# A graph layer on one Trainium2 core: the in-degree rows by one-hot products in the main loop, and five segments of edges in place of four

## What is computed

```python
h = jnp.maximum(_layernorm(x), 0.0)
in_deg = jnp.minimum(segment_sum(ones, dst, num_nodes), 511)
out_deg = jnp.minimum(segment_sum(ones, src, num_nodes), 511)
sum3d = segment_sum(edge_attr @ W_sum + b_sum, src, num_nodes)
cent_term = sigmoid(centralities @ W_cent + b_cent)
vor_term = sigmoid(voronoi_values @ W_vor + b_vor)
out = x + h + z_in[in_deg] + z_out[out_deg] + cent_term + vor_term + sum3d
```

## Time and profile before

| | |
|---|---|
| three runs | 2472.15, 2475.61, 2476.04 us; median 2475.61 |
| profiled execution, its own time | 2477.0 us |
| its span | 2475.2 us (1.8 us less) |
| main loop | to the last scatter, 2132.4 us |
| first piece of the last segment | 2137.4 us |
| piece 150 of the last segment (first step with a window) | 2259 us |
| last piece | 2457 us |

### The profile page before, as it was taken

How to read it: one execution, slowest core, us unless ns; L and a number is a source line. 1 busy time by engine, 2 the same in 40 slices (tenths; PEclk the granted TensorE clock), 3 DMA queues, 4 the chain that set the end, 5 groups by cost and what they waited for, 6 DMA issues and landing times.

```text
span 2475.2 us, 40112 instructions
## 1 busy us (share of the span) xinstructions
PE 1568.7 (63%) x8689; PEld 1168.9 (47%) x8689; DVE 1655.5 (67%) x5321; ACT 895.0 (36%) x4489; POOL 1852.2 (75%) x1869
## 2 busy tenths in 40 slices
PE   5756666666666432237766765666677766687776
PEld 2234554444454210016555554554565655566655
DVE  8946677878878621549887754444576665698766
ACT  3533333444343533545444433333233333001323
POOL 5777777777777777777777777777777777766786
PEclk7867667766766555559988888777799888899888
DMA  5356544445555553348767776666688777799996
GB/s 141 99 157 197 152 130 129 135 142 158 153 154 156 153 175 106 105 122 234 213 206 213 207 214 187 189 181 183 207 257 236 234 229 216 192 243 222 243 249 187
DMA packets 485071, 451.90 MB, mean 183 GB/s; under 512 B 72407, under 2 KB 444637, under 8 KB 484828
## 3 DMA queue, kind: packets, MB, share of 16 engines
q1 hardware_dynamic: 402782, 300.08, 45.0%
q0 software_dynamic: 78752, 136.44, 17.5%
q10 hardware_dynamic: 3294, 12.80, 1.6%
HBM read 319.28 MB, written 129.59 MB: 181 GB/s over the span
## 4 chain that ended last, share of the span: by engine, by line
POOL 51%; DMA 19%; issue 19%; DVE 4%; PE 3%; ACT 2%; DVEq 1%; SPq 1%; ACTq 0%; POOLq 0%
POOL sorted L528 51%; DMA edge_ring<-in_edge_attr_dram 6%; DMA sorted<-edge_ring,pos_i 6%; DMA edge_ring<-in_L_gnn_z_out_dram,out_i 5%; DMA piece_ring<-sorted 2%; PE bank L1011 2%; ACT junk L863 1%; DVE acc L712 1%; DVE hot_n L685 1%; PE bank L1030 1%; DVE base L800 0%; SPq L423 0%; PE bank L957 0%; DVE gate_normed L751 0%; ACT edge_ring L878 0%
## 5 line engine op out<-in xcount | busy, mean ns | idle before, releaser
L528 POOL DMA_INDIRECT sorted<-edge_ring,pos_i x1660 | 1604.0, 966 | 524.9 <-issue 487.4
L1011 PE MATMUL bank<-piece_ring,hot_n 128*125 128x129 f32 x4920 | 860.6, 326 | 210.3 <-DVE hot_n L685 186.3
L1011 PEld LDWEIGHTS bank<-piece_ring,hot_n 128*125 128x125 f32 x4920 | 772.4, 227 | 348.8 <-DVE hot_n L685 306.3
L685 DVE SCALAR_TENSOR_TENSOR hot_n<-bank,wkey,piece_ring 128x250 f32<-128x250 f32 x1230 | 579.4, 471 | 509.6 <-DMA piece_ring<-sorted 484.6
L863 ACT ACTIVATE junk<-bank,mark_col 128x100 bf16<-128x100 f32 x1664 | 543.4, 337 | 142.9 <-PE bank L988 141.8
L994 PE MATMUL bank<-hot_w,after_b 128*128 128x400 bf16 x416 | 177.6, 427 | 573.6 <-ACT junk L863 568.6
L878 ACT ACTIVATE edge_ring<-key_f 128x5 f32<-128x5 f32 x332 | 69.6, 210 | 1093.3 <-DMA edge_ring<-in_edge_attr_dram 1092.4
L712 DVE TENSOR_TENSOR acc<-bank,acc 125x129 f32 x1230 | 348.3, 283 | 42.5 <-issue 26.5
L994 PEld LDWEIGHTS bank<-hot_w,after_b 128*128 128x128 bf16 x416 | 45.8, 110 | 643.5 <-ACT junk L863 643.3
L863 ACT ACTIVATION_READ_ACCUMULATOR junk<-bank,mark_col 128x1 f32 x1664 | 334.1, 201 | 0.0
L1037 PE MATMUL bank<-hot_dl,hot_dh 128*125 128x100 bf16 x1661 | 199.9, 277 | 27.7 <-DVE hot_dh L620 25.6
(11 more groups left out here) (109 smaller groups left out, 1182.5 us busy)
## 6 DMA issues: line engine op xcount, KB each, us to landing
piece_ring<-sorted SPq DMA_DIRECT2D x1230, 130.0 KB
edge_ring<-in_edge_attr_dram SPq DMA_DIRECT2D x332, 320.0 KB
sorted<-edge_ring,pos_i POOLq DMA_INDIRECT x1660
base<-in_x_dram SPq DMA_DIRECT2D x20, 560.0 KB
out_dram<-base ACTq DMA_DIRECT2D x19, 560.0 KB
out_dram<-base SPq DMA_DIRECT2D x9, 560.0 KB
base<-out_dram SPq DMA_DIRECT2D x9, 560.0 KB
edge_ring<-in_L_gnn_z_out_dram,out_i POOLq DMA_INDIRECT x100, 6.8
```

The lines of the kernel that those rows point to most:

```text
L528: g.indirect_dma_start(rows, bass.IndirectOffsetOnAxis(index, 0), edge_ring[:, slot, at, :], None).then_inc(s_scatter[slot], 16)
L685: v.scalar_tensor_tensor(out=hot_n[:, n % HOT_SLOTS, 0:G, :], in0=iota_ps.unsqueeze(1).to_broadcast([P, G, LOC]), scalar=wkey[:, s % 2, c: ...
L1011: last = t_.matmul(to, hot_n[:, n % HOT_SLOTS, k, :], piece_ring[:, n % PIECE_SLOTS, k, 0:SUM], start=(k == 0), stop=(k == ROW_GROUPS[s] - 1))
```

## The change

It moves the z_in rows into the main loop and cuts the segments anew: 25, 165, 110, 70 and 46 quads. The pieces are 150, 430, 320, 240 and 190 (1330 in all) where they were 150, 470, 360 and 250 (1230); `ahead` is 90 where it was 150. After the histogram is done, the 512 rows of z_in are loaded whole into `dst_parts`, which is free by then. For each window there is a new item `look` in two halves. The first spreads the window's in-degrees over the partitions (one matmul of 125 columns), and VectorE compares them with the numbers of the table's rows (`row_z`), which gives four one-hot tiles of 125 columns in one instruction of 500 numbers a partition. The second multiplies those with the table (four matmuls of 256 columns, float32) and VectorE adds the result to the row in `base`. The planner puts the looks into quads 161 to about 410, moves some node work later, and works in five batches of statistics where there were two. The 100 gathers and 100 additions of z_in in the tail are gone.

```diff
-SEGMENT_QUADS = (25, 185, 130, 76)
+SEGMENT_QUADS = (25, 165, 110, 70, 46)
+TABLE_LEAD = 4
+BATCHES = (0, 45, 55, 70, 85, 100)
...
+        "clear": (0.0, 0.0, 2.5), "node": (2.3, 0.0, 1.3), "look": (0.55, 1.4, 0.0), "piece2": (0.75, 0.66, 0.0)}
...
+            "look": [(0, ("look", k, late)) for k in range(NW) for late in range(2)],
...
-                sp.wait_ge(s_node, (i + 1) * X_WINDOWS)
+                sp.wait_ge(s_z_in, (i + 1) * X_WINDOWS)
...
+                if q == table_quad:
+                    sp.wait_ge(s_count, count_signals(NQ - 1))
+                    sp.dma_start(z_table, z_in.rearrange("(c p) d -> p c d", p=P)).then_inc(s_table_in, 16)
...
-            for kind, w in z_order:
...
+            for w in range(NW):
+                pool.wait_ge(s_out_deg, w // COUNTED + 1)
+                if w >= GATHERS:
+                    pool.wait_ge(s_added, added["z_out", w - GATHERS])
+                g.indirect_dma_start(z_rows[0:NODE_P, w % GATHERS, :], None, z_out[:, :],
+                                     bass.IndirectOffsetOnAxis(out_i[0:NODE_P, w:w + 1], 0)
+                                     ).then_inc(s_z_row[w % GATHERS], 16)
...
+            def look(k, late):
+                if late:
+                    row = base[0:NODE_P, order[k] % ROW_SLOTS, :]
+                    dve.wait_ge(s_look, k + 1)
+                    dve.wait_ge(s_node, k + 1)
+                    v.tensor_tensor(row, ps_look[k], row, ALU.add).then_inc(s_z_in, 1)
+                else:
+                    dve.wait_ge(s_spread, k + 1)
+                    v.tensor_tensor(hot_z[:, k % 2, :, :], ps_degree[k].unsqueeze(1).to_broadcast([P, KZ, LOC]),
+                                    row_z[:, :].unsqueeze(2).to_broadcast([P, KZ, LOC]), ALU.is_equal).then_inc(s_hot_z, 1)
...
+            def look(k, late):
+                if k == 0 and not late:
+                    pe.wait_ge(s_in_deg, 1)
+                    pe.wait_ge(s_table_in, 16)
+                if late:
+                    pe.wait_ge(s_hot_z, k + 1)
+                    for c in range(KZ):
+                        last = t_.matmul(ps_look[k], hot_z[:, k % 2, c, :], z_table[:, c, :], start=(c == 0), stop=(c == KZ - 1))
+                    last.then_inc(s_look, 1)
+                else:
+                    before = [j for j in range(k) if look_bank[j] == look_bank[k]]
+                    if before:
+                        pe.wait_ge(s_z_in, before[-1] + 1)
+                    t_.matmul(ps_degree[k], deg_f[0:NODE_P, order[k]:order[k] + 1].to_broadcast([NODE_P, P]),
+                              ident[0:NODE_P, 0:LOC], start=True, stop=True).then_inc(s_spread, 1)
...
             for q in range(NQ):
                 rank(q)
+                for what, k, late in side[q]:
+                    if what == "look":
+                        look(k, late)
```

More of the change, by code:

```diff
@@ L182, in gnn_kernel @@
                 put(q, todo["stats"].pop(0)[1])
-        for line in ("hist", "node"):
+        for line in ("hist", "node", "look"):
             while q >= KEYS1 and todo[line]:
                 kind, b, part = todo[line][0][1]
-                if kind == "degrees" and NW - len(todo["stats"]) < (GUESTS, NW)[b]:
+                if kind == "look" and (todo["hist"] or q < look_quad or b >= nodes):
+                    break
+                if kind == "degrees" and NW - len(todo["stats"]) < BATCHES[b + 1]:
                     break
@@ L190, in gnn_kernel @@
                 put(q, todo[line].pop(0)[1])
[L191 to L195, removed]
+                if kind == "node" and part % 2:
+                    nodes += 1
+                if kind == "indegrees":
+                    look_quad = q + TABLE_LEAD
+                if kind == "look":
+                    look_bank.setdefault(b, 5 if q < look_end and b % 2 else 6)
+                done = b + 1
+                if kind == "look" and part and done % X_WINDOWS == 0 and done <= GUESTS:
+                    out_quad[done // X_WINDOWS - 1] = q + REST_STORE
+                    x_quad[X_ORDER.index(done // X_WINDOWS - 1)] = q + REST_LOAD
+                if kind in ("node", "degrees") or kind == "look" and not (part and q < look_end - 2):
                     break
-    assert not todo["totals"] and not todo["stats"]
+    assert not todo["totals"] and not todo["stats"] and not todo["look"]
     after = [x[1] for kind in ("piece", "hist", "node") for x in todo[kind]]
+    table_quad = min(look_quad - TABLE_LEAD + 1, NQ - 1)
     side_ahead = [side[q] for q in range(PIECE_AHEAD, NQ)]
@@ L204, in gnn_kernel @@
     ahead = pieces[NS - 1] - SW
-    tail_adds = sorted([(4 + w * (ahead + 20) // ROW_SLOTS if w < ROW_SLOTS
-                         else ahead + BACK_LAG + (w - ROW_SLOTS) * (NW - BACK_LAG - 5) // GUESTS, "z_in", w) for w in range(NW)]
-                       + [(ahead + ADD_LAG + w, "product", w) for w in range(NW)]
+    tail_adds = sorted([(ahead + ADD_LAG + w, "product", w) for w in range(NW)]
                        + [(ahead + Z_LAG + w, "z_out", w) for w in range(NW)])
     added = {(kind, w): n + 1 for n, (_, kind, w) in enumerate(tail_adds)}
[L211 to L216, removed]
     store_start = list(range(0, SW - STORE_WINDOWS + 1, STORE_WINDOWS)) + [SW - 2, SW]
@@ L300, in gnn_kernel @@
         ps_y = bank[6:8]
+        ps_degree = [bank[look_bank[k]][:, D:D + LOC] for k in range(NW)]
+        ps_look = [bank[look_bank[k]][0:NODE_P, 0:D] for k in range(NW)]
         ps_gate = bank[7][0:NODE_P, 0:2 * D]
@@ L789, in add_to_row @@
                     dve.wait_ge(s_guest[(w - ROW_SLOTS) // X_WINDOWS], 64)
-                before = [added[kind_, w] for kind_ in ("z_in", "product", "z_out") if added[kind_, w] < added[kind, w]]
+                before = [added[kind_, w] for kind_ in ("product", "z_out") if added[kind_, w] < added[kind, w]]
                 if before:
@@ L796, in add_to_row @@
                 else:
-                    ring, n, _ = ring_of[kind, w]
-                    places = z_places[ring]
-                    dve.wait_ge(s_z_row[ring][n % len(places)], 16 * (n // len(places) + 1))
-                    last = v.tensor_tensor(row, places[n % len(places)][0:NODE_P, :], row, ALU.add)
+                    dve.wait_ge(s_z_row[w % GATHERS], 16 * (w // GATHERS + 1))
+                    last = v.tensor_tensor(row, z_rows[0:NODE_P, w % GATHERS, :], row, ALU.add)
                 last.then_inc(s_added, 1)
```

62 lines of the change are left out of this document (26 added, 36 removed).

## The result

| | before | changed |
|---|---|---|
| median of four runs | 2473.88 us (2470.49 to 2476.04) | 2383.86 us (2379.61 to 2385.67) |
| span of the profiled execution | 2475.2 us | 2382.4 us |
| last scatter | 2132.4 us | 2133.7 us |
| first piece of the last segment | 2137.4 us | 2138.7 us |
| 100 steps begin, last piece | 2258.8, 2457.0 us | 2197.8, 2363.2 us |

The ratio is 0.9631, 95% interval 0.962 to 0.9643: 90 us faster, where 2396 was forecast.

A forecast was written before the change was run, and what follows sets the result against it. POOL's scatters were taken to bound the loop, with a tail of pieces and steps after it: first piece 2137.4, plus 2, 62, 175 and 18, is 2394.4, and 1.8 between span and time gives 2396 us, range 2370 to 2435.

The forecast's parts named there:

- The bound: Main loop: POOL's scatters alone set the pace, 5.06 us a quad to 2132 us; side work fits, adding 2 us.
- The lead: End of the loop: the last quad's index is written 28 us before its last tile goes out, absorbing overruns.
- A look on PE: Main loop: products 1.9 us and spread 0.25 to 0.35, together 2.2 us of PE a look.
- Tail, first part: Tail ahead of the 100 steps: 90 pieces at 0.64 us plus 4, 62 us (53 to 73), for 122.
- a slow start: First part of the tail: 4 us added for the slow start of the ring.
- The 100 steps: Tail, after the first part: 175 us for 198, ends 150 (POOL alone) and 198 (nothing won).
- Where guests come back: In the 100 steps: DMA is full, 17 z_in gathers go and 9 us count, 90 us for 45 steps.
- The other 55: Steps outside the guest stretch: 15 gathers go, saving 22 us if POOL bounds, 8 if DMA; 14 taken, 85 us.
- The second rival: In the 100 steps: they do not shorten, the z_out loop bounds them at 1.98 us; 2419 us, chance 0.12.
- end: After the 100 steps: 18 us as before, nine steps without pieces.
- The slower one: Main loop: gaps keep PE's clock low; at a mean of 0.6, 2547 us, slower than before near 0.63; chance 0.04.
- The loop pays a part: Main loop: side work meets, the lead is used up, POOL waits for indices; +24, 2418 us, chance 0.12.

The follow-up runs named there:

- Experiment 7: The changed kernel with the body of its looks taken out, z_in rows left out of the sum: 2382.09 us against 2475.4 for the kernel before, ratio 0.9626.
- experiment 6: The changed kernel with most guest rows not brought back, with z_out rows added 11 steps after their pieces, and with both: 3005.42, 3019.12, 3011.27 us against 3050.21.
- experiments 1 to 3: Looks without new segments; new segments on the kernel before, without looks; changed kernel with look products made twice, thrice: first-run ratios to before 0.9895, 0.9984, 0.9985, 1.0041.

## Why the prediction was right

*The bound.* POOL's pace held: the last scatter 1.3 us later than before, for a forecast of 2. Experiment 7 shows that this is not luck of two errors: with the looks gone it is 2.0 us earlier than with them. The lead shrank by 0.8 us. In the three stretches of the loop PE had 3.3, 3.9 and 4.0 us of work a quad and VectorE 2.4, 4.0 and 3.4 (busy share times 5.06), where the sums said 3.2 to 4.0. A look on PE was 2.6 us and not 2.2 (products 2.2 for 1.9, spread 0.42 for 0.3). On VectorE it was 1.09 us, forecast 1.1.

*Tail, first part.* 59 us for a forecast of 62, 0.66 a piece. The closeness is in part luck. The term taken was DMA's work, 0.64 a piece, and DMA was not full: a share of 0.75 over 58 us and 89 pieces is 0.49. VectorE was the busy one, 52.5 of 58 us, with two instructions a piece that start every 0.58 to 0.59 us when nothing holds them; the forecast had that figure as its lower end. Of the 4 us for a slow start about one showed (the first ten pieces took 7.2 us, most other tens 6.2 to 6.6).

*The 100 steps.* 165 us for 175, and this is the mis-sized term. It had two parts. Where guests come back it put 45 steps at 90 us, on the ground that DMA is full there and only the 9 us of 17 z_in gathers come off. DMA's work was priced well: 1.05 x 86 us is 90. But it was done in 86 us, for 46 steps. That DMA is what sets this stretch was not shown; on a disturbed chip the steps kept their length when most of the guest rows were left out (experiment 6). The other 55 it put at 85 us, midway between POOL alone and DMA alone; there are 54, and they took 26 + 53 = 79. The first 20 run at 1.31 us each, below POOL's 1.50: a z_out row is added nine steps after its piece, so nine of them add none, the other additions waited 1.7 us in all, and only 15 gathers stand beside them (the first at 2202.1). The last seven gathers come after the last piece. The forecast had priced every step with a gather. The second rival, steps bound by the landing of z_out rows, would have given 198; VectorE's wait for them fell from 50 to 32 us. The rule quoted from the Trainium skill, "DMA: Bandwidth & Descriptors", "Anatomy of one DMA — SWDGE (gpsimd) path", gives an estimate of 2.3 us for such a DMA, and steps down to 150 us. The trace after disagrees as the one before did:

```profile
DMA to landing us min/median/max: 3.6/7.5/12.1
```

*Sum.* Against the forecast of 2396.2: loop -0.7, first part -2.9, steps -9.6, end 19.2 for 18, which is +1.2. That is 2384.2 us, the profiled execution's time.

*The rivals.* The slower one, PE at its lower clock in the loop, had its point at a mean of 0.63; no stretch of the table came under 0.80 (in stretches of 100 us the lowest is 0.76), and it was the looks themselves that raised the clock from 0.50 to 0.80. "TensorE: Matmul & The Clock Gate", Part 1, of the Trainium skill says that the throttled state is the default and activity releases it; the two rows agree.

*The loop pays a part* did not come true in the runs that were forecast (POOL's waits for an index: 31 us). It came true on the disturbed chips, and not by a quad too full, but by PE, ScalarE and VectorE waiting for one another, which the rival names as a reason for it, with signals of PE that come late. There the same change is worth 0.85% and not 3.7%. The forecast had no price for a loop that POOL does not set.

## What to carry to other kernels

Where one engine sets a loop at a fixed pace of its own issue, work for the others can be free: a hundred looks, 263 us of PE, cost 2 us here, and how much more would fit was not measured. The tail behind the loop is a sum whose terms can be priced one by one: this forecast came within 12 us by that. Ask how thin the cover is: a change that moves 105 us out of the tail into covered time is worth only a quarter of it once the hand-overs between the covered engines take longer. Judge a result beside the kernel before on the same chip, and look at the place of the last loop instruction and at the tail apart; a piece ahead of the steps took 0.62 to 0.66 us in every trace of a kernel without z_in gathers in its tail, and the 100 steps 161 to 173, whatever the total was.

## What was not expected of the hardware

The same program, the kernel before, took 2474 us or 3002 to 3053, with durations that outside PE differ by 7% at most in the costliest groups and the same number of DMA packets (402782 of its largest queue in both traces). What differed were the signals of PE, arriving several together and in a twentieth of the recorded ones of L1010 close to ten microseconds or more after the product's modelled end. The chip is not the cause by itself: one chip gave 3049.91 us for the kernel before beside the first runs of experiments 1 to 3 and 2475.4 beside the last. What delays the signals stays open; no run took it apart.

Added work raised the clock by much: in the 200 us from 800 on PE's matmul instructions went from 213 to 536 and its busy time from 70 to 129 us, and the granted clock from 0.50, which is nearly always 1.2 GHz, to 0.80. The looks paid part of their own cost in this way: beside them the products of the pieces have 64 us less of busy time (833.6 for 897.2), and those of `rank` and `rebase` 24 less (497 for 520).
